# Two experts of a mixture layer computed ahead of the expert loop

## The reference, cut to what matters

```
logits = x @ gate_w.T
probs = jax.nn.softmax(logits, axis=-1)
top2_w, top2_idx = jax.lax.top_k(probs, 2)
cap = int(CAPACITY_FACTOR * T / E)                 # 1.25 * 4096 / 8 = 640
counts = jnp.bincount(top2_idx.reshape(-1), length=E)
keep = (counts <= cap).astype(x.dtype)
comb = zeros((T, E)).at[arange(T)[:, None], top2_idx].add(top2_w) * keep[None, :]
h = jax.nn.relu(jnp.einsum('th,ehf->tef', x, W1) + b1[None, :, :])
y = jnp.einsum('teh,ehf->tef', h, W2) + b2[None, :, :]
out = jnp.einsum('te,tef->tf', comb, y)
```

## Time and profile before

| | us |
|---|---|
| median of three executions | 598.16 |
| the profiled execution, whole | 596.94 |
| its span, first to last instruction | 595.1 |
| TensorE busy (4516 products) | 575.1 |
| VectorE busy | 483.7 |
| ScalarE busy | 372.0 |
| GpSimd busy | 288.1 |
| mean granted clock of TensorE | 0.989 |

### The profile page before, as it was taken

The page is one execution under the profiler, slowest core; times in us unless marked ns, Lnnn a source line. Parts: engine busy times, 40 slices in busy tenths (PEclk is TensorE's granted clock), DMA queues, the critical chain, the costliest instruction groups (busy, mean ns, idle before and its releaser), DMA issues. The chain is left out here.

```text
span 595.1 us, 15251 instructions
## 1 busy us (share of the span) xinstructions
PE 575.1 (97%) x4516; PEld 492.3 (83%) x4516; DVE 483.7 (81%) x1026; ACT 372.0 (63%) x855; POOL 288.1 (48%) x248
## 2 busy tenths in 40 slices
PE   8999999999999999999999999999998997799998
PEld 8888888888888888888888888888887896466775
DVE  4235888898989898988889898989898788777776
ACT  1767767777777677777777767777775321534443
POOL 1011666666666666666666666666666563000000
PEclk9999999999999999999999999999999977999999
DMA  7300000000000000000000000000000000000004
GB/s 240 86 2 2 1 3 2 0 0 0 0 0 0 0 0 0 0 0 0 0 0 0 0 0 0 0 0 0 0 0 2 1 1 0 1 1 0 0 0 141
DMA packets 9364, 7.18 MB, mean 12 GB/s; under 512 B 1089, under 2 KB 8833, under 8 KB 9217
## 3 DMA queue, kind: packets, MB, share of 16 engines
q1 hardware_dynamic: 9344, 6.94, 3.9%
HBM read 4.84 MB, written 2.10 MB: 12 GB/s over the span
## 5 line engine op out<-in xcount | busy, mean ns | idle before, releaser
L1068 POOL TENSOR_TENSOR pair<-kx 128x1152 f32<-128x1152 f32 x32 | 82.2, 2568 | 167.4 <-DVE shifted L388 158.4
L580 PE MATMUL bank_a<-v,prob 128*128 128x65 f32 x1024 | 128.5, 274 | 1.5 <-ACT prob L814 0.8
L580 PEld LDWEIGHTS bank_a<-v,prob 128*128 128x128 f32 x1024 | 121.8, 192 | 6.3 <-ACT prob L814 3.2
L1063 POOL TENSOR_TENSOR mix_hi<-mix_hi 128x512 f32<-128x512 f32 (+2 forms) x96 | 116.8, 1217 | 7.5
L271 DVE TENSOR_REDUCE row_max<-bank_s 128x4 bf16<-128x512 f32 x128 | 88.9, 694 | 26.2 <-PE bank_s L555 25.3
L814 ACT ACTIVATE prob<-bank_t 128x512 f32<-128x512 f32 x128 | 68.9, 589 | 6.9 <-PE bank_t L570 4.7
L587 PE MATMUL misc<-yT,wq_sb 128*128 128x128 f32 x512 | 69.6, 279 | 0.5 <-DVE yT L419 0.5
L570 PE MATMUL bank_t<-qT,kT 64*128 64x256 f32 x512 | 65.7, 376 | 0.0
L1056 POOL TENSOR_TENSOR mix_hi<-weight,kx 128x1024 f32<-128x1024 f32 x32 | 64.1, 2002 | 3.1 <-ACT weight L814 3.1
L282 DVE TENSOR_TENSOR att<-bank_a,recip_den 128x256 f32<-128x256 f32 x128 | 54.4, 425 | 13.0
L587 PEld LDWEIGHTS misc<-yT,wq_sb 128*128 128x128 f32 x512 | 62.0, 191 | 3.6 <-DVE yT L419 0.7
(11 more groups left out here) (149 smaller groups left out, 998.9 us busy)
## 6 DMA issues: line engine op xcount, KB each, us to landing
out<-acc_all SPq DMA_DIRECT2D x8, 256.0 KB, 2.3
x_all<-in_xT SPq DMA_DIRECT2D x1, 1024.0 KB, 9.7
w_sb<-in_w SPq DMA_DIRECT2D x2, 512.0 KB
x_all<-in_xT SPq DMA_DIRECT2D x1, 768.0 KB, 7.5
wq_sb<-in_wq SPq DMA_DIRECT2D x1, 512.0 KB, 6.1
wpost_sb<-in_wpost SPq DMA_DIRECT2D x1, 512.0 KB, 9.6
x_all<-in_xT SPq DMA_DIRECT2D x1, 256.0 KB, 3.3
b_rows<-in_b SPq DMA_DIRECT2D x16, 4.0 KB
```

Source lines behind the costliest of these rows:

```text
L580: last = mm(att_bank(g)[:, w, :], prob[:, g % 2, w, :], v1[:, j, g, :], start=(w == 0), stop=True, skip_group_check=True)
L1063: G.tensor_tensor(mix_hi[:, 0:r, :], mix_hi[:, 0:r, :], mix_hi[:, r:2 * r, :], ALU.add).then_inc(s_hi, 1)
L1068: G.tensor_tensor(pair[:, :, :], bass.AP(kx2, jc * 2 * P, [[4 * P, P], [0, SHIFTS], [1, P]]), bass.AP(kx2, jc * 2 * P, [[4 * P, P], [MD, S ...
```

## The change

After the logits of 24 batches (slot 31) the first choices are counted per expert, and the two experts with the fewest are picked in slot 32 (`pick_ahead`; equal counts by index). Both are computed for all 32 batches while the drain runs, in 16 units of one expert and one quad: a hidden product, a relu, four output products and a copy to `ahead_out`. The last quad of both stands at the end, since its tokens come last. The units take the place of the fillers. The transposes of `x1` for `acc_all`, of which half stood before the routing, come after all units.

The loop runs over the kept experts that were not picked, at least three passes. If a picked expert turns out not to be kept, its gates are zero, and the other kept experts are all in the loop. In the first two passes ScalarE scales tiles of `ahead_out` by their gates, three after each relu; GpSimd scales four quads of the second picked expert, adds the two experts' results, and adds the sum to `acc_all` quad by quad. In the second pass VectorE waits for that addition before it adds to a quad (`s_added`). The additions of the second bias move into the first pass. The order and the number of passes are worked out before the gates.

In all batches the mix of rows 0 to 7 is now written with the rows innermost and summed by one reduction instead of three additions, and `mix_hi` has two buffers. In the last three slots VectorE, not ScalarE, makes the two copies of scores. The sums of batch s - 3 follow the scores of the last batches in slots 33 and 34.

```diff
...
-EARLY, RECENT = range(BATCH - QUAD), range(BATCH - QUAD, BATCH)
+AHEAD = 2
+EARLY, RECENT = range(BATCH - 2 * QUAD), range(BATCH - 2 * QUAD, BATCH)
...
+        SCALED = [(x, t) for q in range(QUADS) for x in range(1 if q < QUADS // 2 else AHEAD)
+                  for t in range(q * QUAD, (q + 1) * QUAD)]
...
+            def pick_ahead():
+                dve.wait_ge(s_cnt1_mm, 1)
+                ROUTE_STEPS["count1_read"] = step(V.scalar_tensor_tensor(
+                    out=key[:, :], in0=misc[0][:, 0, 0:EXPERTS], scalar=float(EXPERTS), in1=index8[:, :],
+                    op0=ALU.mult, op1=ALU.add))
+                ROUTE_STEPS["pick"] = ranked(ahead_order)
+                step(V.tensor_scalar(not_ahead[:, :], place[:, :], float(AHEAD), None, ALU.is_ge))
...
-                if D:
-                    dve.wait_ge(s_lo, 4 * d + 1)
-                    V.tensor_tensor(mix_lo[:, 0:4, :], mix_lo[:, 0:4, :], mix_lo[:, 4:8, :], ALU.add).then_inc(s_lo, 1)
...
-                    dve.wait_ge(s_lo, 4 * d + 3)
-                    V.tensor_tensor(mix_lo[:, 0, :], mix_lo[:, 0, :], mix_lo[:, 1, :], ALU.add).then_inc(s_lo, 1)
...
+                def own_copies():
+                    if H:
+                        dve.wait_ge(s_score, n(h))
+                        V.tensor_reduce(score[:, 1:MH // 2, MH:2 * MH], score[:, 1:MH // 2, 0:MH].unsqueeze(3), AX.X,
+                                        ALU.max).then_inc(s_twice, 1)
...
+                    heads_max(s, 3)
+                if D:
...
+                    dve.wait_ge(s_lo, 2 * d + 1)
+                    V.tensor_reduce(mix_part[:, :], mix_lo[:, :, :], AX.X, ALU.add).then_inc(s_lo, 1)
...
-                if s_is(s, BATCH + 1):
-                    dve.wait_ge(s_log, 1)
-                    dve.wait_ge(s_const, 3)
-                    first_choice(EARLY)
+                if s_is(s, BATCH):
+                    own_copies()
+                if s_is(s, BATCH + 2):
+                    second_choice(EARLY, 1)
...
+                if s_is(s, BATCH - 1):
+                    dve.wait_ge(s_log, 1)
+                    dve.wait_ge(s_const, 3)
+                    first_choice(EARLY)
...
+                if s_is(s, BATCH - 1):
+                    ROUTE_STEPS["count1"] = step(V.tensor_reduce(count[:, :], part(first, EARLY).rearrange("p t e -> p e t"),
+                                                                 AX.X, ALU.add))
...
+            dve.wait_ge(s_cnt_mm, 1)
+            step(V.tensor_scalar(keep[:, :], misc[0][:, 0, 0:EXPERTS], float(CAP), None, ALU.is_le))
+            step(V.tensor_tensor(keep_loop[:, :], keep[:, :], not_ahead[:, :], ALU.mult))
+            step(V.scalar_tensor_tensor(out=key[:, :], in0=keep_loop[:, :], scalar=-float(EXPERTS), in1=index8[:, :],
+                                        op0=ALU.mult, op1=ALU.add))
+            ROUTE_STEPS["order"] = ranked(order)
+            step(V.tensor_reduce(kept[:, :], keep_loop[:, :], AX.X, ALU.add))
+            step(V.tensor_scalar(n_run[:, 0:1], kept[:, :], 3.0, None, ALU.max))
+            ROUTE_STEPS["n"] = step(V.tensor_scalar(n_run[:, 1:2], kept[:, :], -1.0, 2.0, ALU.add, ALU.max))
...
+            ROUTE_STEPS["loop"] = step(V.tensor_tensor(loop_gates[:, :, :], gates[:, :, :], over_t(not_ahead), ALU.mult))
...
+            for q in range(QUADS):
+                dve.wait_ge(s_gate_now, 1)
+                dve.wait_ge(s_x1n, q + 1)
+                dve.wait_ge(s_e_mm, q + 1)
+                for t in range(QUAD):
+                    tile = q * QUAD + t
+                    V.scalar_tensor_tensor(out=acc_all[:, tile, :], in0=bank_e[q % 2][:, t, :],
+                                           scalar=gate_run[:, 0, tile:tile + 1], in1=acc_all[:, tile, :],
+                                           op0=ALU.mult, op1=ALU.add).then_inc(s_e, 1)
+                for done in ((q,) if q < QUADS // 2 else (2 * q - 8, 2 * q - 7) if q >= QUADS - 2 else ()):
+                    add_b2(done)
+            with dve.Fori(1, runs) as k:
                 with dve.Fori(0, QUADS // 2) as two:
                     q = two * 2
                     for i in range(2):
                         dve.wait_ge(s_gate_now, k + 1)
+                        dve.wait_ge(s_added, q + i + 1)
...
+            def pick():
+                pe.wait_ge(s_rt, ROUTE_STEPS["pick"])
+                for x in range(AHEAD):
+                    picked.append(pe.value_load(ahead_order[0:1, x:x + 1], min_val=0, max_val=EXPERTS - 1))
+            def ahead_hidden(u):
+                x, q = unit(u)
+                need(pe, s_ah, u - 1)
+                if q == QUADS - 1:
+                    pe.wait_ge(s_tok, BATCH)
+                pe.wait_ge(s_ah_w1, x + 1)
+                mm(bank_t[u % 2][:, :, :], ahead_w1[:, x, :],
+                   tok_all[:, q * QUAD * P:(q + 1) * QUAD * P], start=True, stop=True).then_inc(s_ah_mm, 1)
+            def ahead_output(u):
+                x, q = unit(u)
+                pe.wait_ge(s_ah, u + 1)
+                need(pe, s_ao, u - 1)
+                for t in range(QUAD):
+                    last = mm(bank_a[u % 2][:, t * P:(t + 1) * P], hT[:, u % 2, t * P:(t + 1) * P],
+                              w2_sb[:, bass.ds(picked[x], 1), :].rearrange("p a f -> p (a f)"),
+                              start=(t == 0), stop=True, skip_group_check=True)
+                last.then_inc(s_ao_mm, 1)
...
                 if s_is(s, BATCH + 2):
+                    ahead_output(9)
+                    ahead_hidden(11)
                     gate_logits(RECENT[:-1])
...
-                    gate_logits(parts_early[0])
+                    gate_logits(EARLY[:12])
                 if s_is(s, BATCH):
-                    gate_logits(parts_early[3])
+                    pe.wait_ge(s_rt, ROUTE_STEPS["count1"])
+                    mm(misc[0][:, 0, 0:EXPERTS], ones[:, :], count[:, :], start=True, stop=True).then_inc(s_cnt1_mm, 1)
+                    pick()
+                    pe.wait_ge(s_ld_ffn, 16 * (3 + P // EXPERTS))
+                    ahead_hidden(0)
+                    ahead_hidden(1)
+                    ahead_output(0)
+                    ahead_hidden(2)
...
                 if s_is(s, BATCH):
-                    gate_logits(parts_early[4])
+                    ahead_output(1)
+                    ahead_hidden(3)
...
                 if s_is(s, BATCH - 1):
-                    gate_logits(parts_early[1])
+                    gate_logits(EARLY[12:])
...
                     if s_is(s, BATCH + 1):
-                        keep_going(40)
-                    if s_is(s, BATCH + 2):
-                        keep_going(12)
+                        for u in range(3, 8):
+                            ahead_output(u)
+                            ahead_hidden(u + 2)
...
                 if s_is(s, BATCH):
-                    gate_logits(parts_early[5])
+                    ahead_output(2)
+                    ahead_hidden(4)
+                if s_is(s, BATCH + 1):
+                    ahead_output(8)
+                    ahead_hidden(10)
+                if s_is(s, BATCH + 2):
+                    ahead_output(10)
...
-                    keep_going(3)
-                if late(s):
                     keep_going(3)
...
+                    ahead_hidden(12)
                     gate_logits(RECENT[-1:])
-                    x1_transpose(range(QUADS // 2))
+                    for u in range(11, UNITS):
+                        ahead_output(u)
+                        if u + 2 < UNITS:
+                            ahead_hidden(u + 2)
...
+            x1_transpose(range(QUADS))
...
+            pe.wait_ge(s_x1n, QUADS)
...
+            pe.wait_ge(s_rt, ROUTE_STEPS["gates"])
+            for i in range(2):
+                src = gates[:, i * 16:(i + 1) * 16, :].rearrange("p t e -> p (t e)")
+                last = nc.tensor.transpose(misc[1][:, i, :], src, ident[:, :])
+            last.then_inc(s_gT_mm, 1)
+            for q in range(QUADS):
+                output(0, q, q % 2)
+                if q + 2 < QUADS:
+                    hidden(q + 2, q % 2)
+                if q == 0:
+                    pe.wait_ge(s_gT, 1)
+                    bias_rows(range(QUADS // 2))
+                if q == 5:
+                    bias_rows(range(QUADS // 2, QUADS))
+            pe.wait_ge(s_w1, 2)
+            for i in range(2):
+                hidden(i, i)
+            with pe.Fori(1, runs) as k:
...
+                act.wait_ge(s_ld_ffn, 16 * (3 + P // EXPERTS))
+                act.wait_ge(s_rt, ROUTE_STEPS["pick"])
+                for x in range(AHEAD):
+                    picked.append(act.value_load(ahead_order[0:1, x:x + 1], min_val=0, max_val=EXPERTS - 1))
+                    f(ahead_w1[:, x, :], w1_sb[:, bass.ds(picked[x], 1), :].rearrange("p a f -> p (a f)")).then_inc(s_ah_w1, 1)
...
+            def ahead_relu(u):
+                x, q = unit(u)
+                act.wait_ge(s_ah_mm, u + 1)
```

(90 more changed lines are left out.)

179 lines of the change are left out of this document (94 added, 85 removed).

## The result

The kernel after took 601.86 us (median), beside 597.78 for the kernel before on the same chip: ratio 1.0074, interval 1.0054 to 1.0094. The forecast was 585, with a range to 594. It was wrong: not 2.1% faster but 0.7% slower. The profiled execution has 600.32 us and a span of 598.5, 15.6 more than the predicted 582.9. Three starts, read from the timelines, split the difference; the 31st post product marks the end of the batch loop.

A forecast was written before the change was run, and what follows sets the result against it. TensorE alone was taken to set the batch loop's pace. Span 595.1 - 29.2 (loop) + 12.0 (later loop start) + 5.0 (new wait) = 582.9; with 1.84 outside the span 584.7, given as 585 us, range 576 to 594.

The forecast's parts named there:

- Part 1: Expert loop: two passes of 14.61 us go and the first pass keeps its length, -29.2 us.
- Part 2: Batch loop: 0 us, as TensorE paces; the strided mix_lo product may grow by 1.7 us before it costs anything.
- Part 3: Slots 31 and 32, before the first early product: a chain of steps that puts this product at 484.5 us.
- (b): Slot 31: the first choices for 24 batches on VectorE, before the last normalisations, 4.1 us, bounds 2.0 and 4.5.
- (a): Slot 31: 24 tiles of logits instead of 10, 3.3 to 3.5 us more of TensorE; shift of scores ends at 472.0.
- (d): Slots 31 and 32, TensorE: transposes 0.63, their copy 0.6, post product 2.0, count 0.4; done at 481.2 us.
- Steps (c), (e) and (f): Slots 31 and 32: last two normalisations 1.3 us; ranking 1.9; register loads and weight copy before the first early product 1.4.
- part 4: Drain: TensorE's work from the first early product to the loop's first hidden product sums to 40.5 us.
- part 5: Clock: one stretch of 3.6 us at the lower level, half of it lost, +1.8 us.
- Rival C: Slower: early units come in bursts and the clock stays at 1.2 GHz over them, 24 us more, 609 us; chance 0.04.
- Rivals A, B and D: Well hidden, 577 us (0.20); GpSimd sets the second pass, 594 (0.13); picks not kept, four loop passes, 599.6 (0.01).
- Part 6: Second pass of the expert loop: VectorE's new wait for GpSimd's additions makes a product 5.0 us late, bounds 0 and 9.

The follow-up runs named there:

- a_wait: Kernel after, with GpSimd's additions of the early outputs of the last two quads put behind pass 1 instead of ahead of it: 594.72 us, ratio 0.9942.
- a_wide: Kernel after, with an unused 128-column product before every second of the 24 logits products of slot 31: 606.76 us, ratio 1.0143.
- a_choice: Kernel after, with VectorE's choice for 24 batches put behind the last two normalisations instead of ahead: 598.39 us, ratio 1.0002.
- a_first: Kernel after, with VectorE's choice for 24 batches ahead of the shift that sets off GpSimd's product of pairs: 598.43 us, ratio 1.0012.
- a_x1t: Kernel after, with the x1T addition moved ahead of the reduction of mix_lo: 596.08 us, ratio 0.9959.
- a_xw: Kernel after, with the edits of a_x1t and a_wait together: 591.25 us, ratio 0.9896.

## Why the prediction was wrong

**Part 1, right in sum.** Three passes ran. Pass 0 took 15.53 us, 539.27 to 554.80, for the 16.0 of the forecast, and pass 1 15.71, 1.1 more than the 14.61 booked; the rest was 0.3 shorter. Without the wait the loop took 51.46, and the forecast without its 5.0 had 51.1.

**Part 2 failed, +7.0 us.** The failing step is "it may grow by 1.7 us before it costs anything". It counted VectorE's free time in a slot, an argument on throughput. It left out who stands behind the product on VectorE: x1T, and behind x1T the `x1s` and exponentials on ScalarE, which TensorE needs within the slot. The row had that chain, with ScalarE waiting 1.23 us for x1T, and I used it only for a handover. The product grew by 0.8 us, half of what I allowed, and already cost 0.33 in each of 28 slots. TensorE's 13.99 busy of 14.00 did not speak against this: the kernel after shows 13.98 in slots that are longer, so this share doesn't show waits of that size. Nor does it give the slot's length: from post product to post product the slot of the kernel before is 14.07, not the 13.9 that the prediction names.

The Trainium skill (SBUF — State Buffer, in the section "Door 1: The DMA port swizzle") says that accesses to SBUF run at full rate only while they stay in one line of 16 bytes, four words of fp32. The product's writes are 8 words apart. 1.22 us before and 2.0 after, both with GpSimd in its additions, agree with its direction; I hadn't weighed it.

**Part 3 failed, +6.1 us,** on two terms. (b), the choice: 6.4 us, not 4.1, +2.3. The bounds were 2.0 and 4.5. The failing step is that it scaled the 4.45 us of 28 batches as a whole. Two of its five steps had been held by GpSimd, as these lines of the kernel before show:

```profile
493.36 1.82 DVE L310 TENSOR_TENSOR rest<-logits,r_max 128x224 f32<-128x224 f32 x1
495.21 1.34 DVE L311 SCALAR_TENSOR_TENSOR cand<-rest,rank 128x224 f32<-128x224 f32 x1
...
492.97 1.96 POOL L1056 TENSOR_TENSOR mix_hi<-weight,kx 128x1024 f32<-128x1024 f32 x1 [3.14 <-ACT weight L814]
```

The first ends 0.25 us after GpSimd's product; the second ran beside an addition of 1.29. In the new place the two instructions on GpSimd were longer, 2.56 and 2.08 us, and the two steps, 0.36 with GpSimd idle, became 2.63 and 2.00. The rule of the Trainium skill cited in part 2 covers it: these steps read two tensors from SBUF. The Trainium skill (SBUF — State Buffer, "Summary: rules for kernel authors") adds that of two such instructions the second to issue is blocked until the first has finished; the ends of these steps agree. The other +3.8 are TensorE at 1.2 GHz, for which part 3 booked nothing: about 1.9 ahead of the choice in (a), and 1.9 in (d), where the post product took 3.48 us. (The four terms of (d) add up to 3.6; the times use 3.8.) Steps (c), (e) and (f) came out as booked, within 0.1.

**Parts 4 and 5, right.** From the first early product to the loop it was 41.66 us for 42.3. TensorE was at 1.2 GHz for 2.9 us of it, which costs half, so 40.2 stand against the 40.5 of part 4 and 1.5 against the 1.8 of part 5. In the other nine kernels that ran the units the drain took 41.7 to 44.7, with 3.0 to 9.1 us at 1.2 GHz, and less half of these it is 40.1 or 40.2 in each. What part 5 left out is the clock in slots 31 and 32, ahead of the drain. The check that the prediction set itself, a start before 520 or after 534, was met by 539.27. Rival C had the clock low over the units: in the kernel after it was for 2.9 us. In a_wait, a_wide, a_choice and a_first it was for 8.1 to 9.1, past the 8 us named as the sign of C, but this cost 4 to 5 us, not 24. Rivals A, B and D are out as well: the wait came, GpSimd's steps stayed under 1.5 us, three passes ran.

**Part 6, right.** Two waits, at quads 6 and 7, worth 5.3 us by a_wait for 5.0 booked. What was missing is what follows: after 1.73 and 2.96 us of idle time TensorE ran 5 us at 1.2 GHz, +2.4.

**What stays open.** How much of the start is the clock's has no experiment of its own. The kernels after, a_wait, a_x1t and a_xw run the same instructions in slots 31 and 32, and took 32.3, 31.7, 35.2 and 31.1 us, so this part varies by 4 us from run to run. In them the clock first fell 4.5, 9.9, 5.2 and 10.2 us behind the post product's start. What sets this moment isn't known, nor what makes the time at 1.2 GHz in the drain vary.

## What to carry to other kernels

Free time on an engine prices an edit only if nothing waits for what is queued behind it: ask of each lengthened instruction which result comes next on its queue, and by when another engine needs it. A run that moves that one result earlier and one that moves it later show where the corner is. A choice or ranking made of tiny VectorE steps must not stand beside long GpSimd instructions: here it was three times longer, and moving it ahead of them gave back 0.6% in the kernel after, and 1.2% in the one with the two other edits.
